# Attention and expert layer on one core: a batch's projections made two batches ahead, its K and Q loaded a stage early, x and z normalised on POOL

## What is computed

```python
# x: 16 batches x 512 tokens x 128 channels; Wq, Wk, Wv: 128 x 128; 16 heads of 8 channels
mod = (silu(c) @ wmod).reshape(16, 6, 1, -1)          # sa, ca, ga, sb, cb, gb for each batch
h = layernorm(x) * (1 + ca) + sa
Q, K, V = (h @ W.T).reshape(16, b, s, 8)              # each of Wq, Wk, Wv; heads are slices of tokens
out = softmax(Q @ K.T) @ V
y = out + h
x = x + ga * (y - mean(y over batch's s, d)) / sqrt(var(y) + 1e-5)
h = layernorm(x) * (1 + cb) + sb
# 8 experts of width 256, all computed densely, the two with the highest gate logits weighted:
x = x + gb * sum_e w_e * ((silu(h @ w1_e + b1_e) * (h @ w2_e + b2_e)) @ w3_e + b3_e)
```

## Time and profile before

| | before |
|---|---|
| median of 3 runs | 1536.86 us (1528.1 to 1540.64) |
| the profiled execution | 1535.74 us |
| its span, first to last instruction | 1533.9 us |
| PE busy | 1355.0 us (88%) |
| DVE busy | 1151.3 us (75%) |
| ACT busy | 855.6 us (56%) |
| POOL busy | 279.8 us (18%) |
| stages 2 to 15, from one y_stats to the next (13 periods) | 50.4 us each |
| the experts' half | about 900 to 1534 us |

### The profile page before, as it was taken

One profiled execution on the slowest core, in us unless ns is written; L12 is line 12 of the kernel. 1 busy time (PEld: TensorE's weight loads), 2 busy tenths in 40 slices (PEclk: granted clock), 3 DMA queues, 4 the chain that ended last, 5 costly groups with the idle time before them and its releaser, 6 DMA issues.

```text
span 1533.9 us, 24345 instructions
## 1 busy us (share of the span) xinstructions
PE 1355.0 (88%) x8445; PEld 735.2 (48%) x8445; DVE 1151.3 (75%) x2821; ACT 855.6 (56%) x1590; POOL 279.8 (18%) x411
## 2 busy tenths in 40 slices
PE   2697888888878888888888899999999999999998
PEld 1121222122212222222221258888888888888887
DVE  4587888898888888887898437766676766677775
ACT  2067787788887787877787753333333333333332
POOL 3221332233213331332121111000000000000000
PEclk9999999999999999999999799999999999999999
DMA  8346465556555565646552210000000000000000
GB/s 157 78 76 121 89 127 116 105 119 128 121 112 122 116 131 114 118 107 125 110 112 64 75 44 23 16 16 17 16 16 16 16 16 16 17 16 14 11 11 13
DMA packets 355834, 108.93 MB, mean 71 GB/s; under 512 B 282448, under 2 KB 338176, under 8 KB 352640
## 3 DMA queue, kind: packets, MB, share of 16 engines
q1 hardware_dynamic: 343232, 89.81, 29.9%
q10 hardware_dynamic: 12480, 17.57, 3.8%
HBM read 59.88 MB, written 46.67 MB: 69 GB/s over the span
## 4 chain that ended last, share of the span: by engine, by line
PE 65%; DVE 18%; ACT 9%; issue 4%; ACTq 3%; DMA 1%; SPq 1%; POOL 0%; POOLq 0%; DVEq 0%
PE bank L1231 22%; PE bank L1243 15%; DVE neg_max L716 14%; PE bank L1160 10%; PE bank L1135 7%; ACT probs L985 5%; PE bank L1147 4%; ACTq L974 2%; PE bank L1104 2%; PE bank L1107 1%; DMA Kt<-k_dram 1%; PE bank L1191 1%; ACTq L999 1%; PE bank L1180 1%; ACT x_norm L959 1%
## 5 line engine op out<-in xcount | busy, mean ns | idle before, releaser
L716 DVE TENSOR_REDUCE neg_max<-bank 128x1 f32<-128x512 f32 x1024 | 638.3, 682 | 134.3 <-PE bank L1135 132.0
L985 ACT ACTIVATE probs<-bank 128x512 f32<-128x512 f32 x1024 | 539.7, 603 | 165.9 <-PE bank L1147 156.1
L1135 PE MATMUL bank<-Kt,Qt 48*128 48x512 bf16 x1024 | 346.5, 407 | 105.3 <-DVE neg_max L716 56.6
L1231 PE MATMUL bank<-h_part,w_parts 128*128 128x512 f32 x1536 | 384.3, 399 | 3.3 <-DVE hidden L881 3.3
L1066 ACT ACTIVATE gate_act<-bank,b_sb 128x512 f32<-128x512 f32 x256 | 176.4, 689 | 373.8 <-PE bank L1231 373.7
L1147 PE MATMUL bank<-Qt,Kt 51*128 51x512 bf16 x1024 | 339.4, 401 | 25.1 <-ACT probs L985 24.0
L1231 PEld LDWEIGHTS bank<-h_part,w_parts 128*128 128x128 f32 x1536 | 278.2, 188 | 64.8 <-DVE hidden L881 10.2
L881 DVE SCALAR_TENSOR_TENSOR hidden<-bank,b_sb,gate_act 128x512 f32<-128x512 f32 x256 | 190.7, 750 | 136.9 <-ACT gate_act L1066 136.4
L1135 PEld LDWEIGHTS bank<-Kt,Qt 48*128 48x128 bf16 x1024 | 73.9, 95 | 455.9 <-DVE neg_max L716 364.2
L1160 PE MATMUL bank<-probs,Vt 128*16 128x512 f32 x2048 | 282.2, 624 | 0.1
L1243 PEld LDWEIGHTS bank<-w_sb,hidden 128*128 128x128 f32 x2048 | 247.1, 192 | 8.9
(11 more groups left out here) (123 smaller groups left out, 797.7 us busy)
## 6 DMA issues: line engine op xcount, KB each, us to landing
o_dram<-o_sb ACTq DMA_DIRECT2D x64, 256.0 KB, 3.9
q_dram<-q_parts SPq DMA_DIRECT2D x48, 128.0 KB, 4.5
k_dram<-k_parts SPq DMA_DIRECT2D x48, 128.0 KB, 11.6
Qt<-q_dram SPq DMA_DIRECT2D x32, 192.0 KB
Kt<-k_dram SPq DMA_DIRECT2D x32, 192.0 KB
x_in<-in_x SPq DMA_DIRECT2D x16, 256.0 KB, 3.1
h_dram<-hT SPq DMA_DIRECT2D x16, 256.0 KB, 3.7
Qt<-q_dram SPq DMA_DIRECT2D x32, 128.0 KB
```

What stands on the lines that cost most here:

```text
L716: dve.tensor_reduce(neg_max[:, side, a, col:col + 1], score_a[m % 3][:], AX_X, ALU.max, negate=True).then_inc(s_max, 1)
L985: act.activation(probs[:, 4 * (j % 2) + (k ^ 1)], score_b[n % 3][:], ACT.Exp).then_inc(s_exp, 1)
L1135: pe.matmul(score_a[m % 3][:], Qt[b % BUFS][first:first + ROWS, n, P * c:P * c + P], Kt[b % BUFS][first:first + ROWS, n], start=True, stop ...
L1231: ins = pe.matmul(up_bank[2 * c + k][:], w[:, i, e, P * c:P * c + P], h_parts[par][j], start=(i + j == 0), stop=(i == 1))
```

## The change

- `misc_uses`: the front made in stage b is that of batch b+2, with its four products in steps 3, 4, 6 and 11 in place of 0, 2, 3 and 4. Stage 0 makes the fronts of batches 1 (steps 0 to 3) and 2 (steps 6, 7, 8, 11).
- SP: q, k and v of batch b+1 were stored in stage b-1, so stage b can load them at once. `q_load` and `v_load` now stand right behind `x2_store`, ahead of `inv_store` and `inv_load`; `k_load` follows these, then all stores of the front of b+2, then `back_load`. The stores wait in addition until the loads of the batch before have landed, since DRAM holds one batch's q, k and v.
- x_norm moves from ACT to POOL (`x_normal`: subtract the mean, multiply by rstd), one batch further ahead; DVE's `front_shift` goes from the stages. z moves from ACT to POOL (`y_normal`, with y_scale computed there too) and DVE's `end_shift` goes, for all batches but the last.
- POOL: `add_h` of batch b-2 now stands ahead of the splits of q and k, the new normalisations at the stage's end.

```diff
--- before.py
+++ after.py
@@ -40,14 +40,21 @@
 DMA = 16
+FRONT = ("x_turn", "q", "k", "v")
+
+
 def misc_uses(b):
     uses = [
-        (0, "x_turn", b + 1, 0), (1, "max_rows", b - 1, 1), (2, "q", b + 1, 0), (3, "k", b + 1, 0),
-        (4, "v", b + 1, 0), (8, "mean", b - 2, 0), (9, "max_rows", b, 0), (10, "var", b - 2, 0),
-        (15, "z_turn", b - 2, 0),
+        (1, "max_rows", b - 1, 1), (8, "mean", b - 2, 0),
+        (9, "max_rows", b, 0), (10, "var", b - 2, 0), (15, "z_turn", b - 2, 0),
     ]
-    return [u for u in uses if 0 <= u[2] < NB]
+    uses += [(q, what, b + 2, 0) for q, what in ((3, "x_turn"), (4, "q"), (6, "k"), (11, "v"))]
+    if b == 0:
+        uses = [u for u in uses if u[2] == 0]
+        uses += [(q, what, 1, 0) for q, what in enumerate(FRONT)]
+        uses += [(q, what, 2, 0) for q, what in zip((6, 7, 8, 11), FRONT)]
+    return sorted(u for u in uses if 0 <= u[2] < NB)
 def misc_table():
@@ -369,16 +376,19 @@
                     sp.dma_start(h_dram[b], hT[:]).then_inc(s_h_stored, DMA)
                 if what == "q":
                     sp.wait_ge(s_split_q[3], b + 1)
+                    sp.wait_ge(s_q_landed, b * LOADS * DMA)
                     for i in range(PARTS):
                         sp.dma_start(q_dram[i].rearrange("d n g s -> g d n s"),
                                      q_parts[:, i].rearrange("c (n s) -> c n s", s=TOK)).then_inc(s_q_stored, DMA)
                 if what == "k":
                     sp.wait_ge(s_split_k[3], b + 1)
+                    sp.wait_ge(s_k_landed, b * LOADS * DMA)
                     for i in range(PARTS):
                         sp.dma_start(k_dram[i].rearrange("d n g s -> g d n s"),
                                      k_parts[:, i].rearrange("c (n s) -> c n s", s=TOK)).then_inc(s_k_stored, DMA)
                 if what == "v":
                     sp.wait_ge(s_misc_read, misc_index("v", b) + 1)
+                    sp.wait_ge(s_v_loaded, b * 4 * DMA)
                     sp.dma_start(v_dram.rearrange("(t p) c -> p t c", p=P), v_f[:]).then_inc(s_v_stored, DMA)
             def q_load(b):
@@ -467,6 +477,15 @@
                 sp.dma_start(x2[:, par], x2_dram[b].rearrange("(t p) c -> p t c", p=P)).then_inc(s_x2[par], DMA)
                 sp.dma_start(gb_all[:, par], gb_dram[bass.ds(b, 1)].broadcast_to([P, D])).then_inc(s_x2[par], DMA)
+            def front(b):
+                for what in FRONT:
+                    front_store(b, what)
+
+            def loads(b):
+                q_load(b)
+                v_load(b)
+                k_load(b)
+
             def stage(b, par):
                 if b == NB:
                     sp.wait_ge(s_x2_stored, 2 * DMA)
@@ -474,24 +493,26 @@
                     sp.wait_ge(s_b, (NB - 1) * STEPS)
                     f_load(0, 0)
                     f_load(1, 1)
-                if has(b, 0, NB - 3):
-                    x_load(b + 2)
+                if b == 0:
+                    x_load(2)
+                    front(1)
+                    loads(1)
                 if has(b, 2, NB + 1):
                     x_back_load(b - 2)
                 if has(b, 3, NB + 2):
                     x2_store(b - 3)
-                if has(b, 0, NB - 2):
-                    front_store(b + 1, "x_turn")
+                if has(b, 1, NB - 2):
+                    q_load(b + 1)
+                    v_load(b + 1)
+                if has(b, 0, NB - 4):
+                    x_load(b + 3)
                 if has(b, 2, NB + 1):
                     inv_store(b - 2, par)
                     inv_load(b - 2, par)
-                if has(b, 0, NB - 2):
-                    front_store(b + 1, "q")
-                    front_store(b + 1, "v")
-                    q_load(b + 1)
-                    front_store(b + 1, "k")
-                    v_load(b + 1)
+                if has(b, 1, NB - 2):
                     k_load(b + 1)
+                if has(b, 0, NB - 3):
+                    front(b + 2)
                 if has(b, 1, NB):
                     back_load(b - 1, 1 - par)
@@ -585,10 +606,29 @@
                 pool.wait_ge(s_x_ve, b + 1)
                 pool.tensor_tensor(x_rstd[:], x_ve[:], neg_half[:], ALU.pow).then_inc(s_x_rstd, 1)
+            def x_normal(b):
+
+                pool.wait_ge(s_x_rstd, b + 1)
+                pool.wait_ge(s_misc_full, misc_index("x_turn", b - 1) + 1)
+                for t in range(TT):
+                    pool.tensor_scalar(x_norm[:, t], x_in[:, t], x_mv[:, t, 0:1], x_rstd[:, t:t + 1],
+                                       ALU.subtract, ALU.mult).then_inc(s_x_norm, 1)
+
             def y_power(b):
                 pool.wait_ge(s_misc_read, misc_index("var", b) + 1)
                 pool.tensor_tensor(y_rstd[:], y_ve[:], neg_half[:, 0:1], ALU.pow).then_inc(s_y_rstd, 1)
+
+            def y_normal(b):
+
+                pool.wait_ge(s_y_rstd, b + 1)
+                if b:
+                    pool.wait_ge(s_z, b)
+                pool.tensor_tensor(y_scale[:], mod[:, 2, b:b + 1], y_rstd[:], ALU.mult).then_inc(s_y_scale, 1)
+                pool.wait_ge(s_y_scale, b + 1)
+                if b:
+                    pool.wait_ge(s_misc_full, misc_index("z_turn", b - 1) + 1)
+                pool.tensor_scalar(z[:], y[:], y_mean[:], y_scale[:], ALU.subtract, ALU.mult).then_inc(s_z, 1)
             def add_h(b):
@@ -616,17 +656,27 @@
                     f_power(0)
                 if has(b, 0, NB - 1):
                     relay_v(b, par)
-                if has(b, 0, NB - 2):
-                    split_q(b + 1)
-                    split_k(b + 1)
+                if b == 0:
+                    split_q(1)
+                    split_k(1)
+                    x_power(2)
+                    x_normal(2)
                 if has(b, 2, NB + 1):
                     add_h(b - 2)
+                if has(b, 1, NB - 3):
+                    split_q(b + 2)
+                    split_k(b + 2)
                 if has(b, 0, NB - 1):
                     split_max(b, 0)
-                if has(b, 0, NB - 3):
-                    x_power(b + 2)
+                if b == 0:
+                    split_q(2)
+                    split_k(2)
+                if has(b, 0, NB - 4):
+                    x_power(b + 3)
+                    x_normal(b + 3)
                 if has(b, 2, NB + 1):
                     y_power(b - 2)
+                    y_normal(b - 2)
             x_power(0)
             pool.wait_ge(s_x_rstd, 1)
@@ -692,12 +742,14 @@
             def front_stats(b, tiles):
                 if tiles[0] == 0:
                     dve.wait_ge(s_x_in, (b + 1) * DMA)
+                    if b >= 2:
+                        dve.wait_ge(s_x_norm, TT * b)
                 for t in tiles:
                     dve.bn_stats(x_stats[:, t], x_in[:, t]).then_inc(s_x_stats, 1)
             def front_shift(b):
                 dve.wait_ge(s_x_rstd, b + 1)
-                if later(b):
+                if b:
                     dve.wait_ge(s_x_norm, TT * b)
                 dve.scalar_tensor_tensor(x_shift[:], x_mv[:, :, 0], -1.0, x_rstd[:], ALU.mult, ALU.mult)\
                     .then_inc(s_x_shift, 1)
@@ -732,6 +784,8 @@
             def end_dev(b):
                 dve.wait_ge(s_misc_full, misc_index("mean", b) + 1)
+                if b:
+                    dve.wait_ge(s_z, b)
                 dve.tensor_copy(y_mean[:], end_bank(b)[:, 0:1]).then_inc(s_misc_read, 1)
                 dve.wait_ge(s_misc_read, misc_index("mean", b) + 1)
                 dve.tensor_tensor(y_dev[:], y_mv[:, 0:1], y_mean[:], ALU.subtract).then_inc(s_y_dev, 1)
@@ -822,13 +876,14 @@
             def stage(b, par):
                 for r in range(QUADS):
-                    if has(b, 0, NB - 3):
+                    if b == 0 and r == 2:
+                        front_stats(2, range(TT))
+                        aggregate(x_stats, x_mv, x_ve, 2, s_x_stats, s_x_mv, s_x_ve)
+                    if has(b, 0, NB - 4):
                         if r in (8, 9):
-                            front_stats(b + 2, range(2 * (r - 8), 2 * (r - 8) + 2))
+                            front_stats(b + 3, range(2 * (r - 8), 2 * (r - 8) + 2))
                         if r == 10:
-                            aggregate(x_stats, x_mv, x_ve, b + 2, s_x_stats, s_x_mv, s_x_ve)
-                        if r == 13:
-                            front_shift(b + 2)
+                            aggregate(x_stats, x_mv, x_ve, b + 3, s_x_stats, s_x_mv, s_x_ve)
                     if has(b, 2, NB + 1):
                         if r == 2:
                             end_inv(b - 2)
@@ -838,8 +893,6 @@
                             end_dev(b - 2)
                         if r == 11:
                             end_var(b - 2)
-                        if r == 13:
-                            end_shift(b - 2)
                     if has(b, 0, NB - 1):
                         maxima(b, r)
                     if r == 15 and has(b, 2, NB + 1):
@@ -961,7 +1014,7 @@
```

(6 more changed lines are left out.)

## The result

| | before | changed |
|---|---|---|
| median, measured beside each other | 1533.12 us (4 runs) | 1640.6 us (1633.92 to 1659.94, 4 runs) |
| ratio, 95% interval | | 1.068 (1.060 to 1.076) |
| the same once more, for the experiments | 1531.93 us (7 runs) | 1641.49 us (1634.25 to 1645.78, 4 runs), ratio 1.071 (1.066 to 1.077) |
| span of the profiled execution | 1533.9 us | 1643.3 us (execution 1645.14) |

The first row gives all four runs of the changed kernel; the one of 1659.94, a slow one, is left out of the ratio. The change makes the kernel slower by 7%. 1611 had been forecast, 1560 to 1642 the range: right in sign and in the mechanism of a steady stage, 30 us short. The profile after is that of the second measurement.

A forecast was written before the change was run, and what follows sets the result against it. The inverses behind Q's load on SP were to bound each stage: 33.0 + 23.5 = 56.5 us, 6.1 over 50.4, times 13 = 79; with -4 outside these periods, 1535.7 + 79 - 4 = 1611 us, range 1560 to 1642.

The forecast's parts named there:

- third rival: Only the maxima's rows, moved on ACT's queue, are late for PE at step 5: 1551 us; chance 0.05.
- the fourth: POOL as the bound: normalisations over 10 us delay z_turn and the maxima's split, 1640 us and up; chance 0.03.
- the first two: Inverses pass Q's load, about 1480 us, chance 0.08; Q's load quicker without K's stores competing, 1532 us, chance 0.06.
- unhindered period 46.2: Steady stage if nothing else waited: 4.2 us of gains off the 50.4 us period.
- Step 1: o_dram lands 2.4 us after T0, ACT's issue of its last quarter, in place of 7.4.
- Step 2: SP's issues from den's first load take 6.3 us, so Q's loads can start at T0 + 8.7.
- Step 4: Inverses' store, behind the loads of Q, v and x on SP, lands 18.0 us after Q's first issue: T0 + 26.7.
- Step 5: The load of den_inv takes 3.3 us (3.0 to 3.8), to T0 + 30.0.
- Step 6: attn and y on POOL take 2.8 us, to T0 + 32.8; y_stats starts at T0 + 33.0.
- Second part 23.5: y_stats to the next T0: 20.9 before, minus 0.4 of DVE, plus 1.0 for v's product, plus 2.0 for clock or POOL.
- Stage 0, +5: Stage 0 makes two fronts, four products more, partly at half clock: 5 us added.
- it can't pass: The inverses' store uses eight rings including those of Q's loads, so it can't land ahead of Q.

The follow-up runs named there:

- Experiments 1: Changed kernel with SP's store and load of the inverses and the load of x ahead of the loads of Q and v: 1491.6 us, ratio 0.974.
- Experiment 5: Changed kernel with inverses and x ahead of Q and v, and in stage 0 x of batch 3 loaded ahead of batch 1's loads: 1474.65 us, ratio 0.967.
- experiment 4: Changed kernel with one more wait: SP loads Q only once ACT's moves of the maxima's rows have landed: 1691.9 us.
- experiment 3: Changed kernel, same SP order, with Q loaded by twelve DMAs of 8 rows in place of six with broadcasts: 1573.25 us, ratio 1.026.
- experiment 2: Changed kernel with the inverses' store and load issued by ACT, at steps 4 and 7, in place of SP: 1722.65 us.
- experiment 8: Kernel before, with only x_norm and z moved to POOL and DVE's two shifts gone: 1543.26 us, ratio 1.012.

## Why the prediction was right, and where it was short

In the steady stages the mechanism was right and its terms a little small; in stage 0 a step failed. 1640.6 lies 1.4 us inside the upper bound of the range, and 15 us of it come from stage 0, for which the range had no bound, so that it holds is in part luck. The range also leaves out the third rival's 1551 and most of the fourth's 1640 and up, and so not only the first two. By its own steps; means over the 13 batches whose inverses stand behind Q:

- *K's wait and ACT's x_norm and z gone, unhindered period 46.2*: right. Experiments 1 and 5 show it, 46.05 and 45.9. No idle time stands at the stages' starts any more.
- *Step 1, o_dram lands after 2.4*: right, 454.83 - 452.43. *Step 2, Q starts at T0 + 8.7*: 9.1.
- *Step 4, Q0 (Q's first issue) + 18.0, bounds 16.5 and 19.5*: 19.0. It was near the upper case that the step names, in which SP can't issue the store until Q has left the queue: v's four issues hold SP 9.56 us and x's 2.57, and in 11 of the 13 batches the store is issued within 0.2 us of the last event of Q's semaphore (478.44 and 478.38 here). It then lands in 2.8 to 4.8 (478.44 to 481.25 here). **This term was 1.0 too small.**
- *Step 5, 3.3 from rows of an emptier queue*: the loads of den_inv now take 3.3 to 4.1, median 3.8. 0.5 too small. K's load is now issued right behind, but in experiment 1 Q's is, and there it takes 3.0 to 3.6; the reason stays open.
- *Step 6*: attn and y 2.8, right. y_stats at T0 + 34.7 in the mean, 33.0 forecast.
- *Second part 23.5*: 23.5. The half clock is there as forecast, but in two stretches, and the fronts' splits on POOL don't end before T0 + 43. For the maxima's split behind them PE waits in 7 stages, 11.4 us in all; DVE waits 0.5 there in the stage shown. v's product shows as waits of 1.45 and 0.79 us in steps 11 and 12.
- *Period 56.5*: 58.2, so 1.7 too small, all of it ahead of y_stats (steps 2, 4 and 5). Before, the same stages took 50.6 and not the 50.4 of the sum, so the growth is 7.6 where 6.1 had been forecast: times 13, 19 of the 34 us missing in the spans.
- *Stage 0, +5*: +20.3. **Here a step failed, not a size.** The forecast counted the products of the second front and put at nothing, without asking, the one DMA that the move set behind the loads. `x_load(3)` stands behind `front(1)` and `loads(1)` in SP's order, and DVE waits for it at step 8. It could have been read off SP's order, as the forecast had done for the inverses. Experiment 5 puts it at 14 us. That is the other 15 of the 34.
- *Where the stall is*: "DVE idle 5 to 9 us ahead of y_stats" was wrong, 2.4 us stand there and 6.6 at step 5. The third rival had named that wait and the forecast had said that it lies inside the 7 us. It does, as experiment 4 shows, and so the sum didn't change by it.
- *The Trainium skill's rule* that a later DMA on fewer rings may be through first (page "DMA: Bandwidth & Descriptors", section "Queues, rings and completion order"): in the changed kernel neither SP's store nor ACT's two moves passed Q (moves issued at 463.10, last event 478.56, Q's 478.38). In experiment 3, with Q in pieces, the moves did, 436.90 against 440.28. Its other rule, on how many rings a DMA uses ("Why a DMA increments its semaphore by 16 and not by 1"), gives Q's loads of 24, 16 and 8 rows 3, 2 and 8 rings, and each one event more from the issuer. The trace agrees: 32 events for the six loads of each batch, that is twice 4 + 3 + 9, and 108 for the twelve of experiment 3. The store of the inverses has 9, which makes eight rings, and the two moves 8, three rings each; neither is on fewer than three. Which rings they are, no event names. The forecast's "it can't pass" held for the store as a whole.
- *Parts of a landing*: no step of the forecast had asked how much of a transfer waits for Q. The events show that a few parts do and the others don't. In all 13 batches of experiment 2 five of the store's eight parts landed within 2.8 us of its issue, one after 4.5 to 6.6 and the last two after 9.4 to 12.0. In the kernel before, 13 of the 16 parts of k_dram's first store, issued at 477.95, landed after 3.3 us, and the other three at 484.77, 489.71 and 489.94: the forecast's 12.0 is the time of the last three parts in sixteen.
- *x_norm and z on POOL, 1.2 to 4.1 us in all*: mis-sized, and without effect. 3.13 for the four x_norm and 2.08 for z, 5.2 us:

```profile
L614 POOL TENSOR_SCALAR x_norm<-x_in,x_mv,x_rstd 128x128 f32<-128x128 f32 x46 | 36.1, 798 | 1.1
L631 POOL TENSOR_SCALAR z<-y,y_mean,y_scale 128x512 f32<-128x512 f32 x14 | 29.1, 2080 | 1.5
```

The upper bounds, 0.7 for one x_norm and 1.3 for z, came from a cast and an addition of 128x512, 0.62 and 1.26. Measured are 0.80 and 2.08, for z 1.6 times the addition. The cover, 10 us and more, held.

## What to carry to other kernels

When a load is moved forward in a queue, write down what now stands behind it, and who waits for that: here a store of 32 KB, a link in a chain over five engines, was set behind 16 us of load, and taking it out from behind (with the load of x) was worth 150 us, the difference between 7% slower and 3% faster. Ask it also of the first stages, where a program is written out apart and one late transfer isn't hidden by a stage before it. And where two waits lie over each other, taking the shorter one away is worth nothing while the longer stands: the maxima in time gained nothing (experiment 4), and the ACT work taken away was worth 1.6 us a stage with K early and less than nothing with K late.

## What the runs showed of the hardware

- A large load holds small transfers of another queue too. ACT's two moves of 12 KB of maxima, issued 1.2 and 2.0 us behind Q's first load on SP, released PE only 15.5 us later, and the inverses' store on ACT's queue (experiment 2) took about 11 us, where SP's, issued once Q has left the queue, takes 2.8 to 4.8. With the load in twelve pieces of eight rows the moves landed 5.7 us after the second's issue, in time for PE.
- It holds only a part of them: five of the eight parts of that store landed within 2.8 us in every batch, and 13 of the 16 of k_dram's first store, right behind Q, after 3.3 (the events of their semaphores).
- A load that fills the queue shows as length of the issues behind it: Q's six issues took 4.20 us, v's four small ones behind them 9.56, and with Q in pieces 1.94.
- tensor_scalar on POOL with two operands per partition took 0.80 us for 128x128 and 2.08 for 128x512, in the same trace as 0.61 for a cast of 128x512 and 1.26 for an addition.
- At the stages' starts of experiment 8 PE stood for 2.5 to 4.5 us, and the clock was granted at 0.5 in all 14; in the trace of before it stood for 0 to 2.3 us at most of them, and in the stage shown, with 2.00, the clock stayed at 1.00.
